# Attention heads normalised ahead of the output projection, and the two heads of a pair projected together

## The reference

```python
xn = _layernorm(x)                                   # x: 4 batches x 1024 tokens x 128, float32
# attention, 16 heads of 64
normed = xn / l2norm(xn) * sqrt(128) * gamma
q, k, v = split(normed @ w_qkv)                      # w_qkv: 128 x 3072
sim = where(causal, (q * 64**-0.5) @ k.T, -max)      # per batch and head: 1024 x 1024
out = (softmax(sim) @ v) -> (tokens, 16*64) @ w_out  # w_out: 1024 x 128
# beside it: top-2 of 8 experts, 128 -> 512 -> 128, and a layer norm
x = x + attention(xn) + experts(xn)
```

## Time and profile before

| | |
|---|---|
| time, median of 3 runs (lowest, highest) | 1580.72 us (1578.22, 1581.95) |
| the profiled execution: its time, its span | 1578.72 us, 1577.0 us |
| mean granted TensorE clock | 0.968 of 2.4 GHz |
| attention | from about 286 us to the end |
| loop over pairs | rounds of some 158 us |

### The profile page before, as it was taken

How to read it: one execution, slowest core, us unless ns; L and a number is a source line. 1 busy time by engine, 2 the same in 40 slices (tenths; PEclk the granted TensorE clock), 3 DMA queues, 4 the chain that set the end, 5 groups by cost and what they waited for, 6 DMA issues and landing times.

```text
span 1577.0 us, 33357 instructions
## 1 busy us (share of the span) xinstructions
PE 1453.9 (92%) x9130; PEld 1128.0 (72%) x9131; DVE 1076.1 (68%) x2341; ACT 1067.4 (68%) x2590; POOL 904.9 (57%) x923
## 2 busy tenths in 40 slices
PE   3569999599999999999999999999999999999998
PEld 3458888477777777777777777777777777777776
DVE  6655555458866876687658776876687668766883
ACT  2536656277776777777767777777777777777775
POOL 0761000167665766676657666766676667666766
PEclk9669999699999999999999999999999999999999
DMA  8122111111111111111111111111111111111111
GB/s 308 48 83 72 52 58 48 40 38 38 33 28 41 38 33 28 41 38 33 28 39 40 33 28 39 40 33 28 39 40 33 28 40 39 33 28 41 37 28 54
DMA packets 58807, 72.86 MB, mean 46 GB/s; under 512 B 7400, under 2 KB 44560, under 8 KB 58640
## 3 DMA queue, kind: packets, MB, share of 16 engines
q1 hardware_dynamic: 40720, 52.57, 14.0%
q10 hardware_dynamic: 13824, 9.86, 2.0%
q0 software_dynamic: 4096, 8.40, 1.8%
HBM read 20.47 MB, written 16.52 MB: 23 GB/s over the span
## 4 chain that ended last, share of the span: by engine, by line
PE 67%; DVE 6%; issue 4%; ACT 3%; DMA 1%; SPq 0%; DVEq 0%; POOLq 0%; POOL 0%; ACTq 0%
PE max_ps L1291 9%; PE score_ps L1316 8%; PE score_ps L1317 8%; PE misc_ps L1350 8%; PE head_ps L1333 7%; PE head_ps L1337 7%; PE head_ps L1335 7%; PE misc_ps L1267 3%; PE max_ps L1294 2%; PE score_ps L1319 2%; DVE q_a L1125 2%; PE misc_ps L1261 2%; ACT p_hi L1082 1%; PE misc_ps L1300 1%; PE misc_ps L1263 1%
## 5 line engine op out<-in xcount | busy, mean ns | idle before, releaser
L1033 POOL TENSOR_TENSOR p_lo<-probs,p_hi 128x512 fp32r<-128x512 f32 (+3 forms) x768 | 773.7, 1022 | 432.0 <-ACT p_hi L1082 426.2
L1082 ACT ACTIVATE probs<-score_ps 128x512 f32<-128x512 f32 (+3 forms) x768 | 375.3, 489 | 250.8 <-PE score_ps L1319 170.9
L1135 DVE TENSOR_REDUCE row_max<-max_ps 128x1 f32<-128x128 f32 (+7 forms) x512 | 386.8, 756 | 171.6 <-PE max_ps L1294 161.0
L1082 ACT ACTIVATE p_hi<-score_ps 128x512 fp32r<-128x512 f32 (+3 forms) x768 | 373.1, 486 | 0.0
L1333 PE MATMUL head_ps<-p_hi,v_hi 128*65 128x512 f32 (+3 forms) x768 | 295.6, 385 | 0.3 <-POOL p_lo L1033 0.3
L1316 PE MATMUL score_ps<-q_a,k_a 128*128 128x512 f32 (+3 forms) x768 | 267.8, 349 | 14.0 <-issue 10.9
L1317 PE MATMUL score_ps<-q_b,k_b 65*128 65x512 f32 (+3 forms) x768 | 267.3, 348 | 0.0
L1291 PE MATMUL max_ps<-k_a,q_a 128*128 128x384 f32 (+5 forms) x768 | 250.1, 380 | 16.4 <-DVE row_max L1135 12.6
L1337 PE MATMUL head_ps<-p_lo,v_hi 128*65 128x512 f32 (+3 forms) x768 | 259.4, 338 | 0.0
L1335 PE MATMUL head_ps<-p_hi,v_lo 128*64 128x512 f32 (+3 forms) x768 | 259.0, 337 | 0.0
L1316 PEld LDWEIGHTS score_ps<-q_a,k_a 128*128 128x128 f32 x768 | 145.4, 189 | 60.0 <-issue 17.4
(11 more groups left out here) (170 smaller groups left out, 2105.6 us busy)
## 6 DMA issues: line engine op xcount, KB each, us to landing
k_a<-k_a SPq DMA_DIRECT2D x64, 256.0 KB, 3.8
q_b<-q_a SPq DMA_DIRECT2D x64, 256.0 KB, 4.3
sorted_x<-zeros SPq DMA_DIRECT2D x13, 384.0 KB, 16.1
w_raw<-sorted_x SPq DMA_DIRECT2D x26, 192.0 KB, 2.5
sorted_y<-result ACTq DMA_DIRECT2D x78, 64.0 KB, 1.6
acc<-in_L_attn_x_dram SPq DMA_DIRECT2D x4, 512.0 KB, 6.9
w_raw<-in_L_ffn_W_dram ACTq DMA_DIRECT2D x1, 2048.0 KB, 23.1
q_b<-shift SPq DMA_DIRECT2D x128, 2.0 KB
```

The lines of the kernel that those rows point to most:

```text
L1033: pool.tensor_tensor(p_lo[:, slot, 0:w], probs[:, slot, 0:w], p_hi[:, slot, 0:w].bitcast(F32), ALU.subtract).then_inc(p_split, 1)
L1082: ins = act.activation(p[:, (g * CH + c) % RING, 0:width], score_ps[(g * CH + c) % 2][:, 0:width], ACT.Exp, scale=SCALE)
L1135: dve.tensor_reduce(row_max[:, g % 2, t:t + 1], src, axes, ALU.max).then_inc(max_taken, 1)
```

## The change

- ScalarE copies the 65 rows of a finished half to `raw` instead of `heads`. SP then folds the denominator's row (512 numbers on one partition) to 16 partitions with a DMA, VectorE inverts it there (`invert`, two chunks after the half is complete), SP stores it to DRAM, waits until that has landed, and spreads it by a second DMA over 64 partitions (`scale`). VectorE multiplies `raw` by it into `heads` (`normalise`, four chunks after `invert`), the first head of a pair to rows 0 to 63, the second to rows 64 to 127.
- `project_out` takes both heads at once, over 128 rows, with `wo` 128 by 128. A batch of a pair has two units of four tiles: at chunk 6 of the next even head and at chunk 1 of the odd one behind it. VectorE adds a whole bank to `acc` at once.
- `probs` has 4 buffers instead of 6, for the room; ScalarE waits for GpSimd's reading of the one four back. `CUT` goes from 11 to 14.

```diff
-            Y_AT = [6, 9, 10]
-            y_units = [(0, 3), (3, 3), (6, 2)]
+            Y_AT = {(0, 6): 0, (1, 1): 1}
-            CUT = 11
+            CUT = 14
...
-                if g and g < final and c in Y_AT:
-                    order.append(("y", g - 1, Y_AT.index(c)))
-                    order.append(("add", g - 1, Y_AT.index(c)))
+                if g >= 2 and g < final and (g % 2, c) in Y_AT:
+                    order.append(("y", g // 2 - 1, Y_AT[g % 2, c]))
+                    order.append(("add", g // 2 - 1, Y_AT[g % 2, c]))
+                if (at - 6) >= 0 and (at - 6) // CH < final and (at - 6) % CH in LAST:
+                    order.append(("invert", (at - 6) // CH, LAST.index((at - 6) % CH)))
+                if (at - 10) >= 0 and (at - 10) // CH < final and (at - 10) % CH in LAST:
+                    order.append(("normalise", (at - 10) // CH, LAST.index((at - 10) % CH)))
...
+                    def fold_denominator(hp, g, half):
+                        sp.wait_ge(raw_out, n_half(hp, g, half) + 1)
+                        sp.dma_start(den[:, half], raw[HEAD:HEAD + 1, half].rearrange("o (f n) -> o f n", f=FOLD)
+                                     ).then_inc(den_folded[half], 16)
+                    def spread_inverse(hp, g, half):
+                        sp.wait_ge(inverted, n_half(hp, g, half) + 1)
+                        sp.dma_start(inv_rows[half].rearrange("(f n) -> f n", f=FOLD), inv[:, half]
+                                     ).then_inc(inv_stored[half], 16)
+                        sp.wait_ge(inv_stored[half], hp * (16 * G) + (16 * g + 16))
+                        sp.dma_start(scale[:, half], inv_rows[half].partition_broadcast(HEAD)
+                                     ).then_inc(scale_spread[half], 16)
...
+                            if o[0] == "pv" and o[2] in LAST:
+                                fold_denominator(hp, o[1], LAST.index(o[2]))
+                            if o[0] == "invert":
+                                spread_inverse(hp, o[1], o[2])
...
-                                act.wait_ge(pv_done, n_chunk(hp, g, c) + 1 + RING)
-                                act.activation(heads[:, g % 2, cols], head_ps[0:HEAD + 1, cols],
-                                               ACT.Copy).then_inc(heads_out[half], 1)
+                                act.wait_ge(normalised, n_half(hp, g, half) + 1)
+                                act.activation(raw[:, half], head_ps[0:HEAD + 1, cols],
+                                               ACT.Copy).then_inc(raw_out, 1)
...
+                    def invert(hp, g, half):
+                        dve.wait_ge(den_folded[half], hp * (16 * G) + (16 * g + 16))
+                        dve.reciprocal(inv[:, half], den[:, half]).then_inc(inverted, 1)
+                    def normalise(hp, g, half):
+                        cols = slice(half * BANK, (half + 1) * BANK)
+                        i, s = g // 2 % 2, g % 2
+                        dve.wait_ge(scale_spread[half], hp * (16 * G) + (16 * g + 16))
+                        dve.tensor_tensor(heads[s * HEAD:(s + 1) * HEAD, i, cols], raw[0:HEAD, half], scale[:, half],
+                                          ALU.mult).then_inc(normalised, 1)
...
-                            for t in range(tiles):
-                                q0 = (t0 + t) * P
-                            ins = pe.matmul(dst[:, t * (D + 1):(t + 1) * (D + 1)], heads[:, g % 2, q0:q0 + P],
-                                            wo[:, g % 2], start=True, stop=True)
+                        pe.wait_ge(normalised, n_half(hp, 2 * p + 1, n) + 3)
+                        for t in range(GROUP):
+                            q0 = (n * GROUP + t) * P
+                            ins = pe.matmul(dst[:, t * D:(t + 1) * D], heads[:, p % 2, q0:q0 + P], wo[:],
+                                            start=True, stop=True)
```

More of the change, by code:

```diff
@@ L756, in attention_and_experts @@
         pv_done = sem("pv_done")
-        heads_out = [sem(f"heads_out{i}") for i in range(2)]
-        recip_done = sem("recip_done")
+        raw_out = sem("raw_out")
+        den_folded = [sem(f"den_folded{i}") for i in range(2)]
+        inverted = sem("inverted")
+        inv_stored = [sem(f"inv_stored{i}") for i in range(2)]
+        scale_spread = [sem(f"scale_spread{i}") for i in range(2)]
+        normalised = sem("normalised")
         y_added = sem("y_added")
@@ L817, in attention_and_experts @@
             LAG = 4
-            CONSTS = 7
+            CONSTS = 6
             G = BATCH * 2
@@ L870, in beside @@
                     order.append(("weights", 0, 0))
-                if at >= LAG:
+                if at >= LAG and (at - LAG) // CH < final:
                     order.append(("pv", (at - LAG) // CH, (at - LAG) % CH))
@@ L903, in plan @@
                 order = []
-                for at in range(CUT, G * CH + (LAG if last else CUT)):
+                for at in range(CUT, G * CH + CUT):
                     order += beside(at // CH, at % CH, last)
                 if last:
-                    order += [(kind, G - 1, n) for n in range(len(y_units)) for kind in ("y", "add")]
+                    order += [(kind, BATCH - 1, n) for n in range(2) for kind in ("y", "add")]
                 return numbered(order, MISC0)
@@ L981, in walk @@
                                 qkv_weights(sp, hp + 1)
-                            if o[0] == "y" and o[1:3] == (G - 1, len(y_units) - 1) and not last:
+                            if o[0] == "pv" and o[2] in LAST:
+                                fold_denominator(hp, o[1], LAST.index(o[2]))
+                            if o[0] == "invert":
+                                spread_inverse(hp, o[1], o[2])
+                            if o[0] == "y" and o[1:3] == (BATCH - 1, 1) and not last:
                                 sp.wait_ge(misc_ready, n_misc(hp, o[3]) + 1)
@@ L1080, in walk @@
                                 act.wait_ge(pv_done, n_chunk(hp, g, c) + 1)
-                                for p in (probs, p_hi):
-                                    ins = act.activation(p[:, (g * CH + c) % RING, 0:width],
+                                if order is not before_loop or g * CH + c >= PROBS:
+                                    act.wait_ge(p_split, n_chunk(hp, g, c) - PROBS + 1)
+                                for p, ring in ((probs, PROBS), (p_hi, RING)):
+                                    ins = act.activation(p[:, (g * CH + c) % ring, 0:width],
                                                          score_ps[(g * CH + c) % 2][:, 0:width], ACT.Exp,
@@ L1185, in combine, with add_y @@
                         ins.then_inc(comb_step, 1)
[L1187 to L1201 removed]
+                    def invert(hp, g, half):
[7 more added lines that the diff above has]
+                                          ALU.mult).then_inc(normalised, 1)
+                    def add_y(hp, p, n, u):
+                        toks = slice(p * TILES + n * GROUP, p * TILES + (n + 1) * GROUP)
+                        dve.wait_ge(misc_ready, n_misc(hp, u) + 1)
+                        dve.tensor_tensor(acc[:, toks], misc_ps[u % 2][:].rearrange("p (t d) -> p t d", t=GROUP),
+                                          acc[:, toks], ALU.add).then_inc(y_added, 1)
                     dve.sem_inc(pv_done, RING)
                     dve.sem_inc(y_added, 2)
+                    dve.sem_inc(normalised, 2)
                     w_lo(0)
@@ L1216, in walk @@
                                 w_lo(hp + 1)
-                            elif kind == "y":
-                                denominators(hp, g, c, u)
+                            elif kind == "invert":
+                                invert(hp, g, c)
+                            elif kind == "normalise":
+                                normalise(hp, g, c)
                             elif kind == "add":
@@ L1320, in score, with values @@
                         ins.then_inc(scores_ready, 1)
-                    def values(hp, g, c):
+                    def values(hp, g, c, started):
                         half, j, q0 = chunks[c]
@@ L1326, in values @@
                         pe.wait_ge(p_split, n_chunk(hp, g, c) + 1)
-                        if j == 0:
-                            pe.wait_ge(heads_out[half], hp * G + (g + 1))
+                        if j == 0 and (started or g):
+                            pe.wait_ge(raw_out, n_half(hp, g, half) - 1)
                         if c == 0:
@@ L1366, in walk @@
                             elif kind == "pv":
-                                values(hp, g, c)
+                                values(hp, g, c, order is not before_loop)
                             elif kind == "y":
```

63 lines of the change are left out of this document (22 added, 41 removed).

## The result

The changed kernel takes **1836.39 us** (median of 4 runs, 1833.66 to 1840.62) against 1581.34 for the kernel before (4 runs, 1578.22 to 1589.44): a ratio of 1.1606, 95% interval 1.1556 to 1.1656. It is slower, as forecast, but by 255 us where 119 were forecast, and 46 us beyond the range. The profiled execution took 1840.62 us with a span of 1838.9 and a mean granted clock of 0.897 (before: 0.968).

A forecast was written before the change was run, and what follows sets the result against it. TensorE's stream of products was taken to bound the attention phase (busy 136.9 of 140 us). Terms: 1577.0 - 58 + 25 + 138 + 9 + 6 = 1697 us of span, forecast 1700 us, range 1600 to 1790.

The forecast's parts named there:

- TensorE's stream: Output projection on TensorE: a head's products take 0.90 us instead of 1.81, over 64 heads -58 us.
- second unit ahead of the shift: Chunk 1 of odd heads: the shift waits for VectorE's remainder, TensorE stands 0.8 us in 31 heads, +25 us.
- stands at the chain, even, odd and end: TensorE's stalls for the normalisation's DMAs in even heads +138 us and odd heads +9, plus the kernel's end +6.
- The clock: Rival, chance 0.14: TensorE's clock falls in the even heads' stalls, 3 us lost 30 times, 1790 us.
- the case held likeliest: Chance 0.55: the stall as worked out, 1700 us, with its bounds 1637 to 1787.
- The even head's chain: SP's queue behind four copies: store, spread, shift, fold, then VectorE; TensorE stalls 4.6 us, 30 times, +138 us.
- The odd head: Odd heads, without copies: the store ahead holds SP by 1 us, stall 0.3 us, 31 times, +9 us.
- The end: Kernel's end, last ScalarE copy to last store: about 10.2 us instead of 4.5, +6 us.
- Port: VectorE's normalise, both inputs in SBUF: taken at 0.69 us; at 1.56 the sum would be 26 us higher.
- Costed at nothing: VectorE's total work, ScalarE's waits for `p_lo` and `normalised`, peeled chunks and moved loop: no cost.
- The hidden case: Rival, chance 0.13: the waits are hidden; 1529 us with all hidden, 1554 with the odd heads' shift cost.
- Unheld DMAs: Rival, chance 0.15: small DMAs aren't held by the copies; even-head stall 2.5 us, 1637 us.

The follow-up runs named there:

- no chain and the unit in place: Changed kernel without fold, reciprocal, store and spread (normalise multiplies by ones), second output unit moved from chunk 1 to chunk 3 of the odd head: 1557.1 us.
- the same with the chain: Changed kernel with all its work, only the second output unit moved from chunk 1 to chunk 3 of the odd head, behind the shift: 1797.3 us.
- The fillers: Changed kernel with useless TensorE products ahead of each odd head's first scores: 1804.3 us with 12, 1768.9 us with 20.
- Without the chain: Changed kernel without fold, reciprocal, store and spread, normalise multiplying by ones, second output unit still at chunk 1: 1608.0 us.
- the copies were small: Changed kernel with each of the four copies of q and k moving 1 row of 64 inside the loop: 1733.4 us.

## Why the prediction was right in sign and short in size

Four kernels split the result. From before to the one with no chain and the unit in place: -26.5 us (1583.7 to 1557.1). From there to the same with the chain: +240 (1797.3 less 1557.1). Moving the unit ahead of the shift: +39. That makes 1836. The fillers give 67 back, and I put these down to the clock, so 173 of the 240 are left for the stands. The split depends somewhat on its order: the unit's place costs 39 us with the chain and 51 without, and the fillers were tried with the unit ahead of the shift alone.

| term | forecast | measured |
|---|---|---|
| TensorE's stream | -58 | -26.5 |
| second unit ahead of the shift | +25 | +39 |
| stands at the chain, even, odd and end | +138 +9 +6 = 153 | +173 (trace: 138, 38, 6) |
| clock | 0 in the sum | +67 |

- **The clock** is the step that failed. It stood in the prediction as a rival of its own at 0.14, with 90 us. The runs show it as a part of the case held likeliest: the stands come as worked out, and in each of the 30 pairs the clock falls with them. The argument against it, that a score product breaks the stand, fell: in 17 pairs the clock was down before that product began, and the product itself ran at the lower level. By TensorE's busy time the clock stretched the same products by 116 us (1399.9 without the chain and with the unit in place, 1516.2 in the changed kernel); the fillers got 67 of time back. The rule of the Trainium skill ("TensorE: Matmul & The Clock Gate", HAM oscillation), that a wait for DMAs in every round makes each begin at the low clock, agrees with the windows above (0.50 from 1149 to 1155); the page's own case has longer waits, of 3 to 5 us, than the 2.89 here.
- **TensorE's stream** was credited with 31 us too much. The products did get shorter as forecast; the lines of the pages, first the kernel before, then no chain with the unit in place:

```profile
PE 1453.9 (92%) x9130; PEld 1128.0 (72%) x9131; DVE 1076.1 (68%) x2341; ACT 1067.4 (68%) x2590; POOL 904.9 (57%) x923
PE 1399.9 (90%) x8618; PEld 1062.7 (68%) x8619; DVE 1089.4 (70%) x1829; ACT 1066.1 (69%) x2590; POOL 932.4 (60%) x922
```

TensorE is busy 54 us less, for 58 forecast, but the span fell by 25 (1577.0 to 1551.8): it stood 29 us more. That TensorE was busy 97% of the time was read as: what it is spared, the kernel gains. Taking 73 us from it gave 6 in the kernel before; its waits for maxima and at the loop's turn rose from 23.5 to 55.4 us in their place. Other chains (copies, reductions) were just behind it. Which chain takes the rest is only argued: reductions were waited for 29.7 us there, for 12.6 before, and the shift's DMA 12.1 us.
- **Two units ahead of a shift**: the mechanism was right, at 0.8 us a head. It measured 39 in 32 heads, 1.2 each, within the bound of 53. In the changed kernel's trace the wait for `v_lo` is only 7.9 us in all, so the cost there shows at other places; only the move priced it. `CUT` moved with the unit, so a part of the 39 may be the loop's turn: TensorE's waits there went from 17.8 to 5.4 us.
- **The even head's chain** came as worked out: the store held by the copies (4.65 us; alone 1.3), then spread, shift and fold, VectorE idle 6.18 ahead of the reciprocal (forecast about 6), and stands of 138 us in 30 pairs, for 138. That the number was met so closely is in part luck. In the pair shown the chain took 9.59 us from the store's issue to VectorE's end where 8.70 was forecast, but TensorE came to its first stand 0.7 us later than forecast, and its products between the stands took 1.36 us for 0.50, at the lower clock. The waits for the shift (103.7) and the growth of those for maxima (91.8 less 12.6) make 183 us, near the 173 of the table.
- **The odd head** was costed at 0.3 us, 9 in all, and stood 38 us in 28 waits: in the one shown TensorE came earlier than assumed, and one link was longer. That is just over the upper bound given (37). The end took 10.8 us from the last copy to the last store (forecast 10.2). The reciprocal took 0.34, not 0.17.
- **Port**: the lower price was right for most, a median of 0.68 us for `normalise` in the changed kernel, as the earlier trace rows for one input in PSUM; the longest was 1.75 and the odd head above had 1.49. The Trainium skill ("SBUF — State Buffer", SBUF: two separate sides) has VectorE with two SBUF inputs shut out while GpSimd works. The trace agrees with it for some instances, not as the usual case: 13 of 128 took over 0.8 us, and 11 of these began while GpSimd took a difference `p_lo` and ended 0.55 or 0.56 us after it did. GpSimd was at work in half of the span. Without the chain 51 of 128 took over 0.8 us, all begun beside such a difference, and the mean was 1.00.
- **Costed at nothing**: 4 buffers of probs, right. VectorE's total, right: its cut by 64 us gave 7.
- **The hidden case** (0.13): nothing of it appeared. **Unheld DMAs** (0.15): they are held, and even where the copies were small 150 us of loss stayed.

## What to carry to other kernels

A stand of TensorE that comes back each round must be priced with the clock behind it, as here, where stands of 3.7 to 5.7 us brought the lower level 30 times in 30: add what the products behind it lose to the sum itself, not to a rival. Before crediting a shorter stream on an engine that is 97% busy, ask which chain is next and how far behind; here most of the first credit was not to be had. A chain that crosses several in-order queues should be laid out with its latency between the links: here order alone was worth 205 us (39 of them the second unit's place), while taking one wait from one queue was worth nothing.

## What the hardware showed that I hadn't expected

- A small store to DRAM landed 1.3 us after its issue, faster than the fold from partition to partitions inside SBUF (1.7); behind four copies of 256 KB it took 3.9 to 5.7, in 30 pairs.
- Useless products in a stand made the kernel 67 us faster (1836.4 to 1768.9), with the granted clock up from 0.897 to 0.961.
- The long ones of `normalise` ended 0.55 or 0.56 us after the GpSimd instruction beside which they began, 11 of 13 times in the changed kernel.
- Once the clock was down (0.50 from 1149), it stayed down through a score, a second stand and 3 us in which TensorE was busy all the time (1152 to 1155).
